# Last stage of a four-layer transformer kernel: the expert weights are multiplied in before the down product, and PSUM adds the experts

## The reference

```python
x = hidden_states.reshape(-1, D)                       # D = 128
scores = softmax(x @ router_w, axis=-1)                # 8 experts
topk_w, topk_idx = jax.lax.top_k(scores, 6)
g = einsum('td,edf->etf', x, w_gate)                   # f = 64
u = einsum('td,edf->etf', x, w_up)
f_all = einsum('etf,efd->ted', silu(g) * u, w_down)
picked = take_along_axis(f_all, topk_idx[:, :, None], axis=1)
y = sum(picked * topk_w[:, :, None], axis=1)
y = y + silu(h @ ws_gate) * (h @ ws_up) @ ws_down      # the shared expert
# in the layer: h = layernorm(x) * (1 + cb) + sb;  x = x + gb * y
```

## Time and profile before

| | us |
|---|---|
| three runs | 2988.38, 2990.96 (median), 2996.77 |
| the profiled execution | 2990.19 |
| its span, first to last instruction | 2988.5 |
| start of the last phase's first work, after the barrier | 2779.3 |
| last POOL addition of the phase ends | 2978.0 |
| stores are started at | 2979.3 |

### The profile page before, as it was taken

One profiled execution on the slowest core, in us unless ns is written; L12 is line 12 of the kernel. 1 busy time (PEld: TensorE's weight loads), 2 busy tenths in 40 slices (PEclk: granted clock), 3 DMA queues, 4 the chain that ended last, 5 costly groups with the idle time before them and its releaser, 6 DMA issues. The chain is left out here.

```text
span 2988.5 us, 66961 instructions
## 1 busy us (share of the span) xinstructions
PE 2684.0 (90%) x21108; PEld 2310.4 (77%) x21108; DVE 2218.7 (74%) x6614; ACT 1447.0 (48%) x4145; POOL 587.9 (20%) x1034
## 2 busy tenths in 40 slices
PE   6999999998999899999998999779986775999786
PEld 5988888897889699999997999756654553666665
DVE  4888888886777477777776777657769985777797
ACT  3666666665555366666664222234552222555321
POOL 0000000000111000000000111267751115776111
PEclk9999999998999899999999999889995556999898
DMA  4000000002000444444442000075530005554001
GB/s 138 2 2 1 1 1 1 1 1 60 1 0 0 136 149 150 145 147 147 149 145 71 1 0 0 12 228 155 151 100 13 0 0 138 159 151 129 1 0 28
DMA packets 193359, 202.71 MB, mean 68 GB/s; under 512 B 12152, under 2 KB 179336, under 8 KB 191744
## 3 DMA queue, kind: packets, MB, share of 16 engines
q1 hardware_dynamic: 193152, 200.31, 23.3%
HBM read 109.09 MB, written 90.65 MB: 67 GB/s over the span
## 5 line engine op out<-in xcount | busy, mean ns | idle before, releaser
L138 POOL TENSOR_TENSOR hT<-hT 128x256 fp32r<-128x256 f32 x64 | 46.9, 733 | 1468.8 <-ACT hT L131 1468.8
L122 PE MATMUL bank<-hT,a_xA 128*128 128x256 f32 x768 | 228.2, 297 | 5.2 <-ACT a_p L459 2.8
L602 DVE TENSOR_REDUCE a_nmax<-bank 128x2 f32<-128x512 f32 x256 | 174.9, 690 | 57.8 <-PE bank L124 55.6
L123 PE MATMUL bank<-hT,a_xA 128*128 128x256 f32 x768 | 217.4, 283 | 0.0
L124 PE MATMUL bank<-hT,a_xA 128*128 128x256 f32 x768 | 216.9, 282 | 0.0
L1688 ACT ACTIVATE a_p<-bank 128x1024 f32<-128x1024 f32 (+1 forms) x256 | 193.5, 808 | 23.9 <-PE bank L1743 19.7
L1051 ACT ACTIVATE a_p<-a_p,a_nmax 128x256 f32<-128x256 f32 x256 | 128.1, 501 | 135.2 <-DVE a_nmax L1235 135.2
L480 ACT CAST a_xA<-bank 128x256 fp32r<-128x256 f32 x256 | 95.0, 373 | 199.6 <-PE bank L124 199.5
L1316 ACT ACTIVATE f_silu<-bank 128x512 f32<-128x512 f32 x128 | 76.5, 598 | 213.6 <-PE bank L124 213.6
L844 PE MATMUL bank<-arena,f_hidden 128*128 128x128 f32 x1024 | 172.0, 288 | 6.4 <-DVE f_acc L898 5.0
L781 ACT ACTIVATE f_hidden<-bank,arena 128x256 f32<-128x256 f32 x256 | 120.5, 473 | 114.8 <-PE bank L124 113.6
(11 more groups left out here) (286 smaller groups left out, 8600.8 us busy)
## 6 DMA issues: line engine op xcount, KB each, us to landing
pos_dram<-a_pos SPq DMA_DIRECT2D x128, 383.0 KB, 2.4
a_stack<-rows_dram SPq DMA_DIRECT2D x128, 320.0 KB, 4.1
rows_dram<-a_cut SPq DMA_DIRECT2D x192, 192.0 KB, 2.4
a_shifted<-pos_dram SPq DMA_DIRECT2D x128, 256.0 KB, 2.7
gate<-gates_dram SPq DMA_DIRECT2D x32, 256.0 KB, 10.8
arena<-in_task SPq DMA_DIRECT2D x4, 1156.0 KB, 8.2
x<-in_x SPq DMA_DIRECT2D x4, 512.0 KB, 8.5
arena<-in_w SPq DMA_DIRECT2D x1, 2048.0 KB, 7.9
```

What stands on the lines that cost most here:

```text
L122: pe.matmul(out, left[0], right[0], start=start, stop=False, skip_group_check=True)
L123: pe.matmul(out, left[0], right[1], start=False, stop=False, skip_group_check=True)
L602: dve.tensor_reduce(nmax[:, at.ring(2), h, :], s_ps[h][:].rearrange("p (t k) -> p t k", t=NT), AX_X, ALU.max, negate=True).then_inc(s["nma ...
```

## The change

- Layout of the step: the shared expert is now step 0, the four pairs are steps 1 to 4.
- The down product of a pair takes both experts at once: its right side is 128 instead of 256 columns wide, and all five steps of an item add into the same PSUM bank. So that the sum over the experts comes out weighted, `hidden` of steps 1 to 4 is first multiplied, by POOL, with `share`: for each inner feature (partition) and token (column) the weight of that feature's expert.
- `share` has to be made. `cw` (tokens on partitions) is cut by POOL into three bf16 parts that add up to it (four small linked instructions, `split`, in step 4), PE transposes them (step 0), ACT copies them out, PE spreads them with a 0/1 matrix `chosen` over the inner features (four bf16 products of 256 columns, step 1), and ACT copies the two banks out (two copies of 128 x 512, step 2).
- The router of an item runs two items ahead (`i2`) instead of one; `walk` is unrolled over 4 items and starts 10 steps early.
- ACT copies the finished sum to `acc` (step 1 of the item after), POOL adds it to x in step 2 of the item after.
- DVE loses the accumulation and the row statistics. PE does the down product of a step one step later, after the next gate and up products.
- SP stores each item when it is added (16 transfers of 128 KB); the block with four transfers goes.

```diff
 @block.sync
+    for i in range(NB):
+        sp.wait_ge(s["added"], i + 1)
+        sp.dma_start(k.out[i]..., n.x[:, i]).then_inc(k.stored, 16)
+    sp.wait_ge(k.stored, 16 * NB)
 @block.gpsimd
+    def split(at):
+        wait(pool, s["cw"], at, item=True)
+        wait(pool, s["partsT_mm"], at.shift(-PER), item=True)
+        link(pool.tensor_tensor(parts[:, :, 0, :], c, zero[:], ALU.add), 1)
+        link(pool.tensor_tensor(rest[:], c, parts[:, :, 0, :], ALU.subtract), 2)
+        link(pool.tensor_tensor(parts[:, :, 1, :], c, parts[:, :, 0, :], ALU.subtract), 3)
+        pool.tensor_tensor(parts[:, :, 2, :], rest[:], parts[:, :, 1, :], ALU.subtract).then_inc(s["parts"], 1)
+    def step(at):
+        i2, pi = at.shift(2 * PER), at.shift(-PER)
+        if at.p and at.real:
+            wait(pool, s["hidden"], at)
+            wait(pool, s["share"], at, 2, 1 - (at.p - 1) // 2, item=True)
+            wait(pool, s["y_mm"], at.shift(-2))
+            pool.tensor_tensor(scaled[:, r, :], hidden[:, r, :], share[..., at.p - 1, :], ALU.mult)
+        if at.p == 4 and i2.real:
+            split(i2)
+        if at.p == 2 and pi.real:
+            residual_by_pool(pool, n, pi, acc[:, pi.s // PER % 2], ...)
 @block.scalar     # tanh of nx first, as before
-    if at.p == 1 and ni.real:   # scale and shift
+    if at.p == 1 and i2.real:
...
-    if at.p == 2 and ni.real:   # exponentials
+    if at.p == 2 and i2.real:
...
+    if at.p == 0 and ni.real:
+        wait(act, s["partsT_mm"], ni, item=True)
+        act.copy(partsT[:], partsT_ps)
+    if at.p == 2 and ni.real:
+        wait_scaled(act, at.shift(-PER - at.p + 4))
+        for h in range(2):
+            wait(act, s["share_mm"], ni, 2, 1 - h, item=True)
+            act.copy(share[:, ni.s // PER % 2, 2 * h:2 * h + 2, :], share_ps[:, 512 * h:512 * (h + 1)]...)
+    if at.p == 1 and pi.real:
+        act.copy(acc[:, pi.s // PER % 2], y_ps[pi.s // PER % 2]...)
 @block.tensor     # gate and up products of nx first, as before
+    if at.p == 0 and ni.real:
+        wait(pe, s["parts"], ni, 4, item=True)
+        for t in range(NT):
+            mm = pe.transpose(partsT_ps[:, t * P:(t + 1) * P], parts[:, t]..., k.ident_bf[:])
+    if at.p == 1 and ni.real:
+        wait(pe, s["partsT"], ni, item=True)
+        for h in range(2):
+            for c in range(2):
+                mm = pe.matmul(share_ps[:, 512 * h + c * T:...], chosen[:, 2 * h + c, :], partsT[:], ...)
     # then, for i2: transposes (p == 1), router product (p == 2)
-    if at.real:
-        wait(pe, s["hidden"], at)
-        wait(pe, s["acc"], at.shift(-2), 4)
-        width = P if at.p == LAST else 2 * P
...
+    if b1.real:                 # b1 = at.shift(-1)
+        if b1.p == 0:
+            wait(pe, s["hidden"], b1)
+            wait(pe, s["acc"], b1.shift(-2 * PER), item=True)
+        else:
+            wait_scaled(pe, b1)
+        for t in range(NT):
+            mm = pe.matmul(y_ps[b1.s // PER % 2][:, t * P:(t + 1) * P], (scaled if b1.p else hidden)[...],
+                           w["down"][:, b1.p - 1, :] if b1.p else w["shared"][:],
+                           start=(b1.p == 0 and t == 0), stop=(b1.p == PER - 1))
 @block.vector
-    if at.p == 0 and ni.real:   normalise(... ni ...)
+    if at.p == 0 and i2.real:   normalise(... i2 ...)
     # gated and hidden of nx; hidden now waits for scaled (or y_mm) two steps back
-    if at.real:
-        ...                     # the accumulation, 17 instructions an item
-    if at.p == 3 and ni.real:   softmax_top(... ni ...)
+    if at.p == 3 and i2.real:   softmax_top(... i2 ...)
-    if at.p == 1 and at.shift(-2).real:
-        row_stats(dve, n, at.shift(-2), s["added"])
```

More of the change, by code:

```diff
@@ L375 @@
     ROPE_WEIGHTS[1],
[L376 removed]
+    [("gu", (5, 2, P), P), ("down", (4, P), P), ("shared", (P,), P), ("rw3", (8,), P), ("chosen", (4, P), 24)],
 ]
@@ L664, in build, with store_items, _ @@
             f(nc, d, k)
[L665 to L672, removed]
+        if ffn3 not in phases:
+            store_items(nc, k)
+def store_items(nc, k):
+    with nc.Block() as block:
+        @block.sync
+        def _(sp):
+            for g in range(4):
+                sp.dma_start(k.out.rearrange("b (t p) d -> p b t d", p=P)[:, 4 * g:4 * g + 4],
+                             k.norms.x[:, 4 * g:4 * g + 4]).then_inc(k.stored, 16)
+            sp.wait_ge(k.stored, 64)
 def start_norms(dve, n, s):
@@ L703, in softmax_top @@
     before = at.shift(-at.per)
-    wait(dve, s["acc"], before.shift(-before.p - 1), acc_each)
+    if acc_each:
+        wait(dve, s["acc"], before.shift(-before.p - 1), acc_each)
     if transposed:
@@ L2163, in step @@
                         for t in range(NT):
[L2164 to L2167, removed]
+                            mm = pe.matmul(y_ps[b1.s // PER % 2][:, t * P:(t + 1) * P],
+                                           (scaled if b1.p else hidden)[:, r, t * P:(t + 1) * P],
+                                           w["down"][:, b1.p - 1, :] if b1.p else w["shared"][:],
+                                           start=(b1.p == 0 and t == 0), stop=(b1.p == PER - 1), skip_group_check=True)
@@ L2190, in step @@
                         wait(dve, s["gated"], nx)
-                        wait(dve, s["y_mm"], nx.shift(-2))
+                        if before.p:
+                            wait_scaled(dve, before)
+                        else:
+                            wait(dve, s["y_mm"], before)
                         dve.scalar_tensor_tensor(out=hidden[:, r, :], in0=gated[:, r, :], scalar=0.5,
@@ L2194, in step @@
                                                  ).then_inc(s["hidden"], 1)
-                    if at.p == 2 and ni.real:
-                        wait(dve, s["rt_mm"], ni, item=True)
+                    if at.p == 2 and i2.real:
+                        wait(dve, s["rt_mm"], i2, item=True)
                         dve.tensor_reduce(b["nmax"][:], rt_ps[:, 0:NT * E].rearrange("p (t e) -> p t e", t=NT), AX_X,
                                           ALU.max, negate=True).then_inc(s["nmax"], 1)
-                    if at.real:
[L2200 to L2224, removed]
@@ L2225, in step @@
-                    if at.p == 3 and ni.real:
-                        softmax_top(dve, s, k.spare, ni, E, K, (at.s // PER + 1) % 2, b, acc_each=4, transposed=False)
-                    if at.p == 1 and at.shift(-2).real:
-                        row_stats(dve, n, at.shift(-2), s["added"])
-                walk(dve, PER, 2, LEAD, LAG, step)
+                    if at.p == 3 and i2.real:
+                        wait(dve, s["parts"], i2.shift(-2 * PER), 4, item=True)
+                        softmax_top(dve, s, k.spare, i2, E, K, i2.s // PER % 2, b, acc_each=None, transposed=False)
```

122 lines of the change are left out of this document (85 added, 37 removed).

## The result

The changed kernel took 3015.3 us (median of 4 runs, 3014.51 to 3016.5), the kernel before 2992.38 (4 runs, same chip). The ratio is 1.0077, with a 95% interval of 1.0059 to 1.0094: slower by more than the 0.3% that can be told. The profiled execution took 3014.74, its span is 3012.8.

What follows compares the result with a forecast made beforehand. DVE was taken to bound the last phase (11.5 of 12 us an item); afterwards a loop of 11.5 us plus 2.1 for the clock gives 13.6 an item, span 2818.3 + 14 P = 3008.7, time 3010 us (8 in 10: 2980 to 3030).

Steps and rivals of the forecast that it cites:

- The freed DVE time is waiting time: Last phase: DVE loses about 5.4 of 11.8 us an item, but the loop alone is nearly as long as the old item.
- The loop at full clock: Once per item through softmax, POOL's split, PE's transposes and `hidden`: 11.2 us plus 0.3 for shared access, 11.5.
- PE, transposes to gate and up of step 3: PE's part of the loop: transposes, two down products, gate and up, share products and row transposes, 2.66 us.
- hand-over and cuts, to the transposes: POOL's split in the loop: hand-over 0.18, four cuts of 0.23, three links of 0.18, together 1.64 us.
- The shared access: In `softmax_top`, DVE's second scaling can wait for POOL's `scaled` of step 4: 0 to 0.65 us, taken as 0.3.
- The clock: PE's pause of 2.8 us makes its clock fall in every item, for at least 3.4 us; cost taken as 2.1.
- The waits that I named as the sign: PE's longest waits: transposes on POOL's split about 2.8 us an item, gate and up products on `hidden` about 1.6.
- Start and end: Second `cw` at 2794.5, `hidden` of step 4 of item 0 at 2806, tail 6.9 us; span 2818.3 + 14 P.
- Rival 1: PE's clock stays at full speed: pace 11.2 to 11.5 us, time 2977 to 2981 us; chance 0.12.
- rival 2: Clock holds, `softmax_top` loses the full 0.65, small POOL instructions take more: pace 11.9 to 12.5, 2987 to 2995; chance 0.12.
- Rival 3: PE finds the parts ready and busy time sets the pace: 8 to 9.5 us, time 2932 to 2953; chance 0.05.
- Rival 4: POOL's small split instructions cost like big ones (0.73): split 3.6, pace 15.6 us, time 3038; chance 0.05.

Runs made afterwards that it cites:

- filled kernel: The changed kernel with 28 idle bf16 products an item (10 and 18) put in PE's pauses of step 0; 2990.05 us, ratio 0.9993 to the kernel before.
- POOL-held-back run: Changed kernel with the router three items ahead, POOL's step 4 weighting of `hidden` waiting until the softmax has written its top values; 2966.55 us, ratio 0.9924.
- the router three items ahead with its two moves: Changed kernel with the router three items ahead instead of two, share copies moved to step 3 and `softmax_top` to step 4; 2942.64 us, ratio 0.9839.
- the two parts: Changed kernel with the weights cut into two bf16 parts instead of three, two linked POOL instructions instead of four; 2989.41 us, ratio 0.9995.
- the later copies: Changed kernel with ACT's two share copies moved from step 2 to step 3, behind tanh of step 4; 3010.01 us, ratio 1.0062.
- both the later copies and 28 idle products: Changed kernel with the share copies in step 3 and 10 plus 18 idle products in PE's pauses; 2982.1 us, ratio 0.9977.
- three items ahead: Changed kernel with the router three items ahead instead of two, the same instructions otherwise; 2971.97 us, ratio 0.9930, pace 10.7 against 10.0 to 10.5 expected.

## Why the prediction was right, step by step

Forecast were 3010 us, slower, with 3000 to 3029 for this mechanism; measured were 3015.3. The mechanism is the forecast one: a loop at full clock that is as long as the old item, and a fall of the clock in every round of it. Some of its terms are off, and a part of the agreement is luck.

**DVE is relieved, and that alone brings nothing.** Right: 5.9 us in 12 after. "The freed DVE time is waiting time" is what the waits show.

**The loop at full clock, 11.5 us.** The filled kernel measures it, 11.86 in the item shown. By its terms, from one pair of transposes to the next:

| term | predicted | measured |
|---|---|---|
| PE, transposes to gate and up of step 3 (2908.09 to 2911.06) | 2.66 | 2.97 |
| to `hidden`, maximum, exponentials, copies, to the softmax (to 2916.51) | 2.91 + 2.32 | 5.45 |
| softmax with the shared access (to 2918.68) | 1.69 + 0.3 | 2.17 |
| hand-over and cuts, to the transposes (to 2919.95) | 1.64 | 1.27 |
| sum | 11.5 | 11.86 |

Two mis-sized terms nearly cancel, PE's part and the cuts; that they do is luck. The other two are low by 0.2 each. A cut costs 0.22 us, as the line between the rows had given, but four are through in 1.3 with the hand-over, since linked ones follow at 0.30, with 0.08 between them where the prediction took 0.18. PE's part is longer by a short wait that I had not foreseen, before the share products and the row transposes: 0.33 and 0.21 us here, 7.7 and 4.1 us in 12 items of the change, with no releaser that the profile names.

**The shared access, 0.3.** The mechanism was right, the size low: 0.85 in place of 0.36 for the pair is 0.49, in every item from the third softmax on. The order of the two is not open, as I had put it. `hidden` releases both, and POOL starts first. The Trainium skill (SBUF — State Buffer, "Who interferes with whom") has the loser wait for the whole of the other's instruction; the traces agree, and the POOL-held-back run shows that the loser changes with the start and the price remains.

**The clock, 2.1.** Right in size (2.1 measured against the filled kernel) and in place: one fall an item, within 1.1 us of the end of the pause. How it was sized was not right. I took a stretch of the 3.4 us that the trace before shows; 5.1 in the mean were measured, half of which would be 2.6, and that only 2.1 of it reach the pace brings the number back. That is luck. The waits that I named as the sign are shorter too: 2.2 us for the parts and 0.7 for `hidden` in place of 2.8 and 1.6, and the granted clock is 0.81 and not some 0.7. The pace of 13.6 came out at 13.87, and nearly all of that is the loop, 11.74 in place of 11.5. The Trainium skill (TensorE: Matmul & The Clock Gate, "HAM oscillation") would have kept the clock up, since the longest pause was 2.3 us; the trace does not agree, and filling that pause restored 25 us.

**Start and end.** `hidden` of step 4 of item 0 ends at 2806.4, forecast was 2806. The second `cw` is made at 2796.6 and not at 2794.5, so the way from there was put 2 us too long, and again two errors cancel. The tail from the last `hidden` (end 3006.14) is 6.7 us against 6.9, its store 2.8 against 3.1. The span came out 4.1 us above the predicted 3008.7; 14 x 0.27 = 3.8 of this is the pace.

**The rivals.** Rival 1 (clock held) is not what happened, but the filled kernel shows its world: with the pauses gone the time is 2990, not 2977 to 2981. The pace of 11.7 in place of 11.2 to 11.5 is 3 us of that or more, the later start and the idle products in the end are 5; the loop was already as long as the old item. That is rival 2's time, at a pace just below its 11.9. Rival 3 is the world of the router three items ahead with its two moves: pace 9.0, 2942.64. PE's own work is 8.7 us an item there (97.24 in 100 us), where the prediction had added up 7.9. Rival 4 is excluded by the 0.22 us of a cut.

**Where my expectations failed later.** Two misses are of one kind, the two parts and the later copies. With the clock falling in every item, a saving is not worth its length times the items: 0.6 us out of the pause gave 26 us instead of 8, and 0.9 us an item beside the pause gave 0.25. Sizes could be read only in kernels with the clock held. The kernel with both the later copies and 28 idle products missed because the filler was the bound, and the pace three items ahead because I had left out a leg of the loop.

Open: why the low stretch is 3.4 us in some items and 6.8 or 10.2 in others; what the short waits before the share products are; and the 8 us of the stores were seen as one number, the transfer's size was not varied.

## What to carry to other kernels

Before work is moved off the busiest engine, follow one item from the last wait around to itself: where the maker of a value and its first user are neighbours in the order, that loop takes over at once, and the cure is distance (one more item of lead gave 43 us, two moves on top of it 29), not less work. If the new loop has a pause on PE longer than those the trace shows to be harmless, price the clock in every round; and size a step only in a kernel whose clock is held by a filler that leaves PE some room. A saving made in the same change (here the stores, 8 us) can hide a quarter of a loss, so test it alone.

## What was not expected of the hardware

Pauses of about 1.0 us twice an item, with PE busy 82%, left the clock at 1.00; one of 2.0 to 2.3 us, beside a shorter one of 0.5 to 1.0 in most items, brought it to 0.50 in every item. In between lies the kernel before: one pause of 1.7 to 1.9 us an item, and a fall in one of four. Shortening the pause of the change by 0.6 us removed every second fall. A DVE instruction on 8 to 12 elements a partition, 0.17 to 0.23 us by itself, takes 0.5 us or more when it starts beside a POOL multiply of 0.72 us. The kernel with PE filled to 98% with idle products was 25 us faster than the one with PE left to wait.
